# A ninth table looked up by matrix products in three halves, and shorter subtractions on VectorE

## What is computed

```python
e = jnp.stack([tbl_0[ids[:, 0]], ..., tbl_25[ids[:, 25]]], axis=1)      # 2048 x 26 x 128
combined = jnp.concatenate([e, r_dense_x[:, None, :]], axis=1)           # 2048 x 27 x 128
z = jnp.einsum('bfd,bgd->bfg', combined, combined)[:, TRIU_I, TRIU_J]    # 351 products
h = jnp.concatenate([z, r_dense_x], axis=1)                              # 479
h = jnp.maximum(h @ W_top1 + b_top1, 0.0)                                # 512
h = jnp.maximum(h @ W_top2 + b_top2, 0.0)                                # 256
y = h @ W_top3
```

## Time and profile before

| | us |
|---|---|
| timed runs | 517.69, 522.01, 525.85; median 522.01 |
| the profiled execution | 515.37, its span 513.3 |
| PE busy | 414.9 (81%) |
| POOL busy | 282.9 (55%) |
| DVE busy, ACT busy | 247.9 (48%), 232.7 (45%) |
| mean granted clock of TensorE | 0.900 |

### The profile page before, as it was taken

The page is one execution under the profiler, slowest core; times in us unless marked ns, Lnnn a source line. Parts: engine busy times, 40 slices in busy tenths (PEclk is TensorE's granted clock), DMA queues, the critical chain, the costliest instruction groups (busy, mean ns, idle before and its releaser), DMA issues.

```text
span 513.3 us, 8017 instructions
## 1 busy us (share of the span) xinstructions
PE 414.9 (81%) x2976; PEld 385.6 (75%) x2976; DVE 247.9 (48%) x715; ACT 232.7 (45%) x428; POOL 282.9 (55%) x297
## 2 busy tenths in 40 slices
PE   6697739586896979788797979889687877968887
PEld 4586638485895968787797859879687867967786
DVE  7383937434665245542564327533455426721332
ACT  3364516254453635434544435446354346334734
POOL 6666754656464663666546565466536575464210
PEclk9897959798897979999797988989798998997999
DMA  8921221122211121122211222121211222122100
GB/s 225 289 70 36 70 56 27 49 50 69 50 37 46 48 73 38 42 62 67 52 33 47 52 67 58 32 53 52 72 32 47 58 72 53 33 54 54 31 18 6
DMA packets 21488, 30.54 MB, mean 59 GB/s; under 512 B 6986, under 2 KB 15680, under 8 KB 21323
## 3 DMA queue, kind: packets, MB, share of 16 engines
q0 software_dynamic: 9312, 19.00, 14.3%
q1 hardware_dynamic: 11852, 10.83, 8.1%
q10 hardware_dynamic: 287, 0.21, 0.2%
HBM read 26.86 MB, written 0.01 MB: 52 GB/s over the span
## 4 chain that ended last, share of the span: by engine, by line
PE 46%; another core or an unknown queue 27%; ACT 19%; issue 7%; DMA 0%; ACTq 0%; DVE 0%
PE ps_gram L340 16%; PE ps_mlp L349 8%; PE ps_feat L319 7%; PE ps_feat L321 6%; ACT feat L531 5%; ACT z L517 3%; PE ps_feat L283 3%; ACT feat L574 3%; ACT feat L544 2%; PE ps_feat L316 2%; ACT ids_all L568 1%; PE ps_feat L293 1%; ACT stage L547 1%; PE ps_mlp L426 1%
## 5 line engine op out<-in xcount | busy, mean ns | idle before, releaser
L266 POOL DMA_INDIRECT rows<-in_tbl,ids_now x288 | 280.3, 973 | 197.5 <-PE ps_feat L283 76.1
L766 DVE TENSOR_SCALAR hot<-ids_all,row_no 125x256 fp32r<-125x256 f32 x512 | 159.0, 378 | 46.6 <-remote 21.2
L319 PE MATMUL ps_feat<-hot,table_hi 125*128 125x256 f32 x480 | 137.0, 316 | 17.6 <-issue 11.3
L321 PE MATMUL ps_feat<-hot,table_lo 125*128 125x256 f32 x480 | 135.0, 312 | 10.7 <-issue 10.6
L340 PE MATMUL ps_gram<-feat 128*123 128x108 f32 x1024 | 127.1, 281 | 3.8 <-ACT feat L531 3.7
L340 PEld LDWEIGHTS ps_gram<-feat 128*123 128x123 f32 x1024 | 121.9, 196 | 7.6 <-ACT feat L531 4.4
L517 DVE COPY z<-ps_gram 27x208 f32<-27x208 f32 x128 | 46.9, 367 | 156.6 <-PE ps_gram L340 87.0
L319 PEld LDWEIGHTS ps_feat<-hot,table_hi 125*128 125x128 f32 x480 | 105.0, 219 | 19.2 <-issue 10.3
L321 PEld LDWEIGHTS ps_feat<-hot,table_lo 125*128 125x128 f32 x480 | 104.9, 219 | 17.2 <-issue 16.9
L544 ACT COPY feat<-ps_feat 128x256 f32<-128x256 f32 x32 | 19.4, 607 | 143.7 <-remote 94.3
L517 ACT COPY z<-ps_gram 27x208 f32<-27x208 f32 x128 | 41.6, 325 | 94.9 <-remote 48.0
(11 more groups left out here) (73 smaller groups left out, 329.2 us busy)
## 6 DMA issues: line engine op xcount, KB each, us to landing
rows<-in_tbl,ids_now POOLq DMA_INDIRECT x288
table_lo_before<-in_tbl SPq DMA_DIRECT2D x8, 448.0 KB
dense<-in_dense_t SPq DMA_DIRECT2D x8, 128.0 KB
w_lo_before<-in_w SPq DMA_DIRECT2D x1, 1024.0 KB
zp_lo_before<-in_dense_t SPq DMA_DIRECT2D x8, 128.0 KB
zp_lo_before<-z SPq DMA_DIRECT2D x15, 39.0 KB
zp_lo_before<-z SPq DMA_DIRECT2D x15, 36.0 KB
w_lo_before<-in_w SPq DMA_DIRECT2D x1, 512.0 KB
```

Of the source, the lines that this page charges most:

```text
L266: nc.gpsimd.indirect_dma_start(rows[:, row_at(t, f), :], None, gathered[f], bass.IndirectOffsetOnAxis(ap=ids_now[:, t, f:f + 1], axis=0),) ...
L319: nc.tensor.matmul(result, table_hi[:, CHUNK_AT[n] + ch, :], columns, start=first, stop=False)
L321: mm = nc.tensor.matmul(result, table_lo[:, CHUNK_AT[n] + ch, :], columns, start=False, stop=last)
L766: op = nc.vector.tensor_scalar(hot[0:VROWS, u % HOTS, c, :], ids[0:VROWS, k, :], row_no[0:VROWS, no + UNIT * i + c:no + UNIT * i + c + 1], ...
```

## The change

A ninth kept table is added, of 1250 rows (10 chunks, 1280 columns more in each part). It is looked up in halves 1, 2 and 4 alone; in the others it is gathered as before, as the last of the 18. It makes a fifth, single "pair" `LAST`: its ids are spread at the end of an odd tile, its columns are built after `put_dense` of the even tile, and it is looked up between turns 3 and 4 of the even tile. The turns of a tile now have 4, 3, 4, 4 and 3 tables, the last one less where the ninth is looked up. Room is made in SBUF: `y` lies in `hid2`, and `ids_few` lies in `ids_few_no`, so that the ids of the next half may be loaded only when all ids of this one are spread. DVE's subtractions for `zp` and for six of the eight tables are cut into pieces of 256 columns, with copies or comparisons between them.

```diff
-CHUNKS = [8] * 8
+CHUNKS = [8] * 8 + [10]
 KEPT = len(CHUNKS)
+ALWAYS = KEPT - 1
+LOOKED_UP_LAST = (1, 2, 4)
...
-GROUPS = [range(f, min(f + 4, GATHERED)) for f in range(0, GATHERED, 4)]
-TURNS = len(GROUPS)
+GROUP_SIZES = (4, 3, 4, 4, 3)
...
+def group_of(t, n):
+    group = GROUPS[n]
+    return range(group.start, group.stop - (n == TURNS - 1 and t // 2 in LOOKED_UP_LAST))
...
-                      ("ids", h + 1, 1), ("pair", h, 3), ("tile", t, 3), ("tile", t, 4)]
+                      ("ids", h + 1, 1), ("pair", h, 3), ("tile", t, 3), ("pair", h, LAST), ("tile", t, 4)]
...
             def load_ids(h):
                 if h > 0:
-                    sp.wait_ge(ids_few_ready, h)
+                    sp.wait_ge(ids_spread, ids_before(h))
...
             load_dense(0)
-            load_ids(1)
             sp.dma_start(w1_sb[:], w1).then_inc(weights_landed, 16)
...
+            load_ids(1)
             load_dense(1)
+            load_table(sp, ALWAYS)
...
-                for n, group in enumerate(GROUPS):
-                    if turns_before(t, group.stop - 1) > 0:
-                        pool.wait_ge(turned, turns_before(t, group.stop - 1))
+                for n in range(TURNS):
+                    group = group_of(t, n)
+                    if turns_before(t, group[-1]) > 0:
+                        pool.wait_ge(turned, turns_before(t, group[-1]))
...
+            def two_chunks(n, i):
+                if i == 0:
+                    dve.wait_ge(hi_ready, SPLIT_AT[n] + 1)
+                    if n < WHOLE_FIRST:
+                        dve.wait_ge(hot_free, units_before(0, n + 1))
+                chunks = slice(CHUNK_AT[n] + 2 * i, CHUNK_AT[n] + 2 * i + 2)
+                op = rest(table_lo[:, chunks, :], table[:, chunks, :], table_hi[:, chunks, :])
+                if 2 * i + 2 == CHUNKS[n]:
+                    op.then_inc(lo_ready, 1)
...
                         op.then_inc(hot_built, 1)
+                        if split is not None:
+                            two_chunks(split[k], i)
...
+            def rest_chunk(h, c):
+                if h < 0:
+                    return
+                if c == 0:
+                    dve.wait_ge(zp_hi_ready, h + 1)
+                op = rest(zp_lo[h % 2][:, c, :], zp[h % 2][:, c, :], zp_hi[:, c, :])
+                if c == ZP_CHUNKS - 1:
+                    op.then_inc(zp_lo_ready, 1)
...
                 build(h, 3)
                 take(t - 1, 2)
                 put_dense(t)
+                build(h, LAST)
                 take(t - 1, 3)
...
-                rest_zp(h - 1)
-                take(t - 1, 2)
+                rest_chunk(h - 1, 0)
+                take_one(t - 1, 2, 0)
+                rest_chunk(h - 1, 1)
+                take_one(t - 1, 2, 1)
+                rest_chunk(h - 1, 2)
                 put_dense(t)
+                rest_chunk(h - 1, 3)
                 take(t - 1, 3)
...
             build(0, 0)
             build(0, 1)
-            build(0, 2)
-            for n in range(WHOLE_FIRST, KEPT):
-                split_table(n)
+            build(0, 2, (4, 5))
             put_dense(0)
-            build(0, 3)
+            build(0, 3, (6, 7))
```

More of the change, by code:

```diff
@@ L59, with pairs_in @@
 OUTS = 7
+def pairs_in(h):
+    return PAIRS + (h in LOOKED_UP_LAST)
+def group_of(t, n):
+    group = GROUPS[n]
+    return range(group.start, group.stop - (n == TURNS - 1 and t // 2 in LOOKED_UP_LAST))
+GATHERS = [(t, n, f) for t in range(TILES) for n in range(TURNS) for f in group_of(t, n)]
+GATHER_AT = {(t, f): i for i, (t, n, f) in enumerate(GATHERS)}
 def feat_turns():
@@ L70, in feat_turns, with ids_before, landed @@
             order += [("tile", t, 0), ("pair", h, 2), ("tile", t, 1), ("ids", h + 1, 0), ("tile", t, 2),
[L71 removed]
+                      ("ids", h + 1, 1), ("pair", h, 3), ("tile", t, 3), ("pair", h, LAST), ("tile", t, 4)]
         elif h + 1 < HALVES:
             order += [("tile", t, 0), ("tile", t, 1), ("ids", h + 1, 2), ("tile", t, 2), ("pair", h + 1, 0),
[L74 removed]
+                      ("tile", t, 3), ("ids", h + 1, 3), ("pair", h + 1, 1), ("tile", t, 4), ("ids", h + 1, LAST)]
         else:
             order += [("tile", t, n) for n in range(TURNS)]
[L77 removed]
+    return {x: n for n, x in enumerate(x for x in order if x[0] == "tile" or x[1] < HALVES and x[2] < pairs_in(x[1]))}
 FEAT_AT = feat_turns()
+def ids_before(h):
+    return sum(pairs_in(i) for i in range(h))
 def units_before(h, n):
[L85 removed]
+    return (sum(CHUNK_AT[PAIR[pairs_in(i) - 1].stop] for i in range(h)) + CHUNK_AT[n]) // UNIT
 def row_at(t, f):
[L90 removed]
+    return GATHER_AT[t, f] % ROWS
 def turns_before(t, f):
[L95 to L96 removed]
+    at = GATHER_AT[t, f] - ROWS
+    return 0 if at < 0 else TURNS * GATHERS[at][0] + GATHERS[at][1] + 1
+def landed(t, n):
+    return 16 * sum(len(group_of(i, n)) for i in range(t % 2, t + 1, 2))
 def bass_dlrm_tower(nc, dense_t, ids_gathered, ids_kept, gathered, kept, w1, b1, w2, b2, w3, out):
@@ L183, in mlp_bank, with slots @@
             return ps_feat[n] if n in (0, 1) else last_gram[:, n - 2, :] if n in (2, 3) else ps_mlp[at % 2]
+        def slots(p):
+            return (GATHERED - 1, GATHERED) if p == LAST else (GATHERED + PAIR[p].start, GATHERED + PAIR[p].stop)
         def feature(t, first, stop):
@@ L232, in _ @@
             load_ids(0)
-            for n in range(KEPT):
+            for n in range(ALWAYS):
                 load_table(sp, n)
             load_dense(0)
-            load_ids(1)
             sp.dma_start(w1_sb[:], w1).then_inc(weights_landed, 16)
@@ L327, in products @@
                 if b == 0:
-                    pe.wait_ge(emptied, max(FEAT_AT["tile", t, TURNS - 1], FEAT_AT["pair", t // 2, PAIRS - 1]) + 1)
+                    pe.wait_ge(emptied, max(FEAT_AT["tile", t, TURNS - 1], FEAT_AT["pair", t // 2, pairs_in(t // 2) - 1]) + 1)
                     pe.wait_ge(dense_put, t + 1)
@@ L518, in copy_products @@
                           ps_gram[at % 2][32 * j:32 * j + F, :, F * j + 1:F * (j + 1)].rearrange("p c g -> p g c"))
-            op.then_inc(done, 1)
+            if done is not None:
+                op.then_inc(done, 1)
         @block.scalar
@@ L914 @@
     kept = sorted(range(TABLES), key=lambda f: len(tables[f]))[:KEPT]
-    gathered = [f for f in range(TABLES) if f not in kept]
-    order = np.array(gathered + kept + [TABLES])
+    gathered = [f for f in range(TABLES) if f not in kept] + kept[ALWAYS:]
+    order = np.array(gathered + kept[:ALWAYS] + [TABLES])
     arrays = {"in_dense_t": np.ascontiguousarray(x["r_dense_x"].T)}
```

130 lines of the change are left out of this document (73 added, 57 removed).

## The result

The changed kernel takes 539.92 us (median of 4 runs, 535.39 to 543.04) beside 521.36 us (4 runs) for the kernel before: ratio 1.0374, 95% interval 1.0249 to 1.0498. The forecast was 519 us, the range 501 to 533. The profiled execution took 535.39 us, with a span of 533.5.

A forecast was written before the change was run, and what follows sets the result against it. PE was taken as nearest to the bound, its completions reaching others late during unbroken gathers. Terms +7.1 - 4.8 - 1.5 - 4 = -3.2 gave 512.2 us profiled, with 6.6 added 519 us; range 501 to 533.

The forecast's parts named there:

- The ninth table on PE: On PE, in three halves: 60 more matmuls and three spreads, less six transposes, cost +7.1 us net.
- Six gathers fewer: On POOL: six gathers saved, between 2.1 and 7.5 us of gain, taken as -4.8 us.
- The pieces: DVE's cut subtractions hold POOL's gathers for less time: -1.5 us (0 to -5.6).
- The groups 4, 3, 4, 4, 3: POOL's run of ten gathers breaks after seven, but later runs may merge to eleven: -4 us, between -23 and +23.
- The merged runs decide (slower): Rival: eleven gathers in a row beside the lookups of pairs 0 and 1 make PE stand still: 536 us, chance 0.17.
- The broken run decides: Rival: breaking the run of ten gains 23 us over six halves: 500 us, chance 0.28 with milder forms.
- PE alone is the bound: Rival: gathers don't matter, only PE's added work and later layer 1: 529 to 539 us, chance inside the neighbouring cases.
- (1): Sign: POOL's longest runs in a steady half are seven gathers, and eleven where turn 3 came early.
- (2): Sign: the time from batch 3's recorded end to ACT's copy, 8.6 us, falls near 5 if the broken run helps.
- (3): Sign: gathers over 1.5 us near the start are gone, and the mean is below 960 ns.
- (4): Sign: halves 1, 2 and 4 are longer than 3, 5 and 6 by about 1 us.
- (5): Sign: the sum of "remote" waits on ACT, 94.3 and 48.0 us, stays about the same.

The follow-up runs named there:

- e7: The kernel before with a ring of 16 places in place of 14: 402.98 us, ratio 0.9989.
- e18: The kernel before without the gathers of tiles 2 to 15, on a chip where the kernel before takes 516.93 us: 393.75 us.
- e11: The kernel before without the gathers of tiles 2 to 15, on a chip where the kernel before takes some 402 us: 382.48 us.
- e2: The changed kernel with the old sizes of the turns, 4, 4, 4, 4, 2: 521.12 us, ratio 1.0066.
- e9: The changed kernel itself, timed again on a chip where the kernel before takes 402.71 us: 408.1 us, ratio 1.0122.
- e3: The kernel before with only DVE's subtractions cut into pieces: 519.89 us, ratio 1.009.
- e1: The kernel before with only the new sizes of the turns, 4, 3, 4, 4, 3: 548.62 us, ratio 1.0588.
- e16: The changed kernel, each gather waiting for its own place's turn, on a chip where the kernel before takes 523.2 us: 495.36 us, ratio 0.9428.
- e17: The changed kernel with the old sizes and each gather waiting for its own place's turn, beside 516.93 us: 513.15 us, no ratio.
- e5: The kernel before with the new sizes and each gather waiting for its own place's turn, beside 402.50 us: 403.17 us, ratio 1.0014.
- e8: The changed kernel, each gather waiting for its own place's turn, beside 402.50 us: 403.44 us, ratio 1.0022.
- e12: The changed kernel, each gather waiting for its own place's turn, beside 402.71 us: 402.7 us, ratio 1.0001.
- e13: The changed kernel, each gather waiting for its own place's turn, beside 402.51 us: 403.75 us, ratio 1.0034.
- e4: The kernel before, each gather waiting for its own place's turn, beside 516.97 us: 505.94 us, too scattered for a ratio.
- e15: The changed kernel with the old sizes of the turns, beside 523.2 us: 523.64 us, ratio 1.0015.

## Why the prediction was wrong, step by step

*What bounds the kernel.* Right, and it was only an inference then: PE's completions come late while gathers run. In the trace of the kernel before I set PE's semaphore updates against the recorded ends of the matmuls that send them. Of 418 updates 190 come over 0.5 us late; of those whose batch ended inside a run of gathers 156 of 295, outside 34 of 123; and 126 of the 190 arrive 1 to 3 us after the end of a run, 56 of them within 2 us. (Some updates and matmuls are missing from the trace, so updates and ends were paired by the nearest fit.) In e7, on the other kind of chip, none of 476 is late. Without most gathers the time falls by 123 us on such a chip (e18) and by 20 on the other kind (e11), so I put down some 100 us to the lateness. My price of 12.2 us in a half, about 98 in all, was near; a steady half takes 14.6 us more than the 45.0 of e7. What was missing is that this is so on some chips only.

*The ninth table on PE* (+7.1, 2.4 in a half). Borne out: PE's busy time rose by 6.9, and halves 2 and 4, with the lookup, took 2.7 us more than halves 3 and 5 in e2, 2.6 in e9. Its work on DVE and ACT cost nothing that is seen.

*Six gathers fewer* (-4.8). Not seen by itself: the halves with the lookup are longer by all of PE's work, with no gather's gain taken off. Ninth table, gathers, pieces and later ids together make +0.7% (3 us) in e2, where I had +0.8.

*SP's later wait* (0). Right: the only wait of a cast of ids for its DMA is 0.7 us in the whole run.

*The pieces* (-1.5). Wrong in sign: +0.9% (2.5 to 6.9 us) in e3. The rule which I put aside, with 16 comparisons as evidence, was the one to weigh more; mixed with subtractions they kept a gather waiting, and once in e1 even by themselves. PE's wait for the pieces before layer 1, taken at 0 with 10 us as the bound, was 2.1 us in e3 and 7.7 in the kernel after, in two and four waits; halves 3 and 5 of the kernel after lose 1.2 us each there.

*The groups 4, 3, 4, 4, 3* (-4 between -23 and +23). This is the step that failed: +16 us in the changed kernel, +30 in the kernel before (e1). The gain was there as priced, 4.1 us for the shorter wait of the batch, but only in the halves without the lookup; in halves 1, 2 and 4 the run of ten stayed. Two losses stood against it. The first came from "seven gathers to do instead of four" behind turn 2, which I had named but priced only by way of a merge to eleven. It took the gain away: behind turn 2 the kernel after is only 0.3 to 0.5 us quicker than before and 1.1 to 2.4 slower than e2, and e1 is 1.1 to 2.5 slower than before. The second I had at nothing. For the even tile I wrote "seven plus four in place of eight and four" and overlooked that its first run, two tables of which are the last group, grows from six to seven. There the kernel after loses 3.1 us in half 3 and 3.2 in half 5 (3.4 and 2.8 beside e2), and e1 2.0 to 4.4 a half. The merge never came, since turn 3's completion is held back too, and it isn't needed: besides the length of a run it counts how much PE has left to do then that needs no answer. Behind batch 3 PE had layer 1 and the lookups, slow as they went; behind turn 3 it has none (e1, 5.44 us) or 1.9 us of spread and layer 1 (kernel after, 4.21 us), then it waits for ACT. I had read the run of ten as the dearest because its wait was the longest on ACT. But it was ACT and DVE that waited longest there; PE did some of its lookups, and breaking that run gained less than its wait promised.

*The rivals.* "The merged runs decide (slower)", 536 us at 0.17, was nearest in time, right that the seven gathers behind turn 2 cost something, and wrong about the form and about the even tile; its 536 us came from the merge that didn't happen, so the nearness is luck. "The broken run decides" had its effect and was outweighed. "PE alone is the bound" would also have given 529 to 539, and e2 refutes it: all of PE's added work at 1.0066.

*The signs.* (1) Seven in halves 3, 5 and 6, ten as before in halves 1, 2 and 4; eleven no. (2) Near 5 where the run is broken: 4.50 and 4.49 in halves 3 and 5, but 7.8 in halves 2 and 4. (3) No: a mean of 990 ns, not below 960, and a gather of 5.72 us where the longest had been 2.12. (4) No: the halves without the lookup became the longer ones. (5) As forecast, 105.6 and 39.8 together 145.4, against 142.3; so this sum didn't tell the two cases apart.

Still open: why completions are late beside gathers on three of the experiments' five chips (before 516.93 to 523.2) and not on the other two (402.5 and 402.7), whether POOL's instructions or their transfers make them late, what each of the even and the odd tile's new runs costs by itself, and why e16 gains more than e17. The recorded ends of PE are modelled, so the traces can't say whether the matmuls themselves end late or only their signals. The Trainium skill (Perfetto Trace Analysis, section "Tensor Engine Instruction (MATMUL, LD_WEIGHTS)") says as much: the end is an estimate, and the update is sent after the sums are written. It names nothing between the end of the work and the update but the last writes and their acknowledgement. In e7 the update is recorded 0.014 us behind the end (median); a distance of 8.58 us as in the earlier trace rows is not in its account.

## What to carry to other kernels

When a wait of a queue is moved from one signal to another, write down every burst of the queue anew, also those that the change wasn't made for: how long each one gets, what it will stand beside, and how long the engine that it disturbs can go on without an answer. Price all of them, not the longest alone. Let each transfer wait for the place that it needs itself and not a group for the last of its places: by the ratios it cost nothing on the quicker chips (e5, e8, e12; in e13 0.3%), and with the new sizes on a slower chip it took 9% off (e16 beside the changed kernel, by their ratios 0.9428 and 1.0374, which come from different times and perhaps chips). With the old sizes it took off 2% (e4) and 1% (e17 beside e15), both without a ratio. And compare only on one chip: the same kernel differed by 114 to 121 us between the two kinds of chip, and the change cost 1.2% on one kind and 3.7% on the other.

## What was not expected of the hardware

- One kernel, two levels: 402.5 and 402.7 us on two chips, 517.0, 523.2 and 516.9 on three. The difference goes with the indirect gathers: without most of them 382.48 and 393.75 us, and 43.8 us for a steady half on both kinds.
- After its standstills the granted clock is low: 0.50 in the kernel after from 384 to 390 us, and 0.89 to 0.91 over a steady half of the kernel before, against 1.00 in e7 with the same work.
- A gather beside an alternation of 256-column subtractions and pairs of comparisons was held for 5.72 us (kernel after), 6.59 (e3) and 4.86 (e9), each time until the alternation was over, and one in e1 for 5.48 us beside comparisons and then whole subtractions. In the kernel after, on POOL:

```profile
55.30 5.72 POOL L303 DMA_INDIRECT rows<-in_tbl,ids_now  x1 [0.30 <-issue]
61.32 0.95 POOL L303 DMA_INDIRECT rows<-in_tbl,ids_now  x1 [0.30 <-issue]
```
